# Three waits in front of gathers: tiles 3 to 5 of the feed-forward tail wait for the rows two tiles back

## The reference

```python
x = _layernorm(x + _L0_attn_ref(x, ...))            # causal self-attention, 16 heads of 32
x = _layernorm(x + _L0_xattn_ref(x, ctx_2048, ...)) # 16 heads of 128 on 4 key heads, 361 context rows
x = _layernorm(x + _L0_ffn_ref(x, ...))             # 8 experts, 2 per token

def _L0_ffn_ref(x, router_w, router_b, expert_w, expert_b, proj_w, proj_b, norm_w):
    logits = jnp.einsum('bsd,de->bse', x, router_w) + router_b
    topk_vals, topk_idx = jax.lax.top_k(logits, 2)
    topk_w = jax.nn.softmax(topk_vals, axis=-1)
    full_w = jnp.sum(jax.nn.one_hot(topk_idx, E) * topk_w[..., None], axis=-2)
    h = jnp.einsum('td,edf->etf', xf, expert_w) + expert_b[:, None, :]
    combined = jnp.einsum('etf,te->tf', jax.nn.silu(h), full_w.reshape(-1, E))
    y = x + (combined @ proj_w + proj_b)
    rms = jnp.sqrt(jnp.mean(y * y, axis=-1, keepdims=True) + 1e-6)
    return norm_w * (y / rms)
```

## Time and profile before

| | us |
|---|---|
| median of 3 runs | 1625.73 |
| lowest and highest | 1622.57, 1629.63 |
| the profiled execution | 1628.02 |
| its span, first to last instruction | 1626.2 |
| first gather of the tail to the end of the span | 81.1 |
| GpSimd: gathers of tiles 0 to 6 issued | 1545.1 to 1562.4 |
| GpSimd: `rms(0)` | 1564.4 |

### The profile page before, as it was taken

One profiled execution on the slowest core, in us unless ns is written; L12 is line 12 of the kernel. 1 busy time (PEld: TensorE's weight loads), 2 busy tenths in 40 slices (PEclk: granted clock), 3 DMA queues, 4 the chain that ended last, 5 costly groups with the idle time before them and its releaser, 6 DMA issues. The chain is left out here.

```text
span 1626.2 us, 27742 instructions
## 1 busy us (share of the span) xinstructions
PE 1482.5 (91%) x8494; PEld 1217.7 (75%) x8494; DVE 970.8 (60%) x3587; ACT 655.5 (40%) x1762; POOL 639.2 (39%) x994
## 2 busy tenths in 40 slices
PE   7999999999995689999999999999999998479876
PEld 6778878778764478888888888888888887458754
DVE  3666566666664475556655566555665565744468
ACT  4443343344331254443444444344444444433344
POOL 1334333343342364444443444434344342262173
PEclk8999999999998789999999999999999999579988
DMA  6311212212212441112111111211112110756472
GB/s 204 107 67 62 100 60 78 86 58 81 81 51 86 150 132 42 60 54 64 56 45 59 54 59 39 67 59 54 53 42 68 53 43 21 293 139 167 138 223 81
DMA packets 60957, 139.75 MB, mean 86 GB/s; under 512 B 10182, under 2 KB 21034, under 8 KB 59876
## 3 DMA queue, kind: packets, MB, share of 16 engines
q1 hardware_dynamic: 56296, 123.85, 22.9%
q0 software_dynamic: 4576, 14.95, 3.7%
HBM read 94.31 MB, written 44.46 MB: 85 GB/s over the span
## 5 line engine op out<-in xcount | busy, mean ns | idle before, releaser
L913 ACT ACTIVATE b_probs<-b_probs,b_nmax 100x361 f32<-100x361 f32 x256 | 151.9, 593 | 70.7 <-DVE b_nmax L1011 70.4
L65 PE MATMUL b_bank<-b_kTh,b_q 128*100 128x362 f32 x512 | 174.3, 341 | 3.0 <-DVE b_kTl L993 1.7
L1123 POOL TENSOR_TENSOR b_pcarry<-b_half 128x1 f32<-128x1 f32 x176 | 41.7, 237 | 327.5 <-DVE b_rinv L1017 271.7
L1011 DVE CUSTOM_DVE_ANT_0 b_probs<-b_bank,b_mask 100x361 f32<-100x361 f32 x256 | 135.5, 529 | 56.9 <-issue 46.9
L1148 POOL TENSOR_SCALAR b_probs<-b_probs,b_rinv 100x361 f32<-100x361 f32 x256 | 157.4, 627 | 0.0
L1004 DVE TENSOR_TENSOR b_pTl<-b_bank,b_pTh 121x400 fp32r<-121x400 f32 x192 | 110.0, 573 | 52.6 <-ACT b_pTh L908 51.3
L908 ACT ACTIVATE b_pTh<-b_bank 121x400 fp32r<-121x400 f32 x192 | 96.8, 504 | 102.1 <-PE b_bank L754 99.9
L949 ACT ACTIVATE b_oTh<-b_bank,b_bv 128x400 fp32r<-128x400 f32 x64 | 38.1, 595 | 210.2 <-PE b_bank L65 210.2
L754 PE MATMUL b_bank<-b_ident,b_probs 100*121 100x100 f32 x768 | 110.4, 266 | 5.8 <-POOL b_probs L1148 5.8
L754 PEld LDWEIGHTS b_bank<-b_ident,b_probs 100*121 100x121 f32 x768 | 108.4, 187 | 8.2 <-POOL b_probs L1148 7.3
L65 PE MATMUL b_bank<-b_Woh,b_oTh 128*100 128x512 f32 x256 | 108.0, 422 | 1.4 <-DVE b_oTl L1078 1.4
(11 more groups left out here) (241 smaller groups left out, 3981.1 us busy)
## 6 DMA issues: line engine op xcount, KB each, us to landing
q_d<-a_qo SPq DMA_DIRECT2D x64, 400.0 KB, 2.4
b_q<-q_d SPq DMA_DIRECT2D x64, 400.0 KB, 3.1
b_ctxr<-in_ctxT SPq DMA_DIRECT2D x48, 242.0 KB, 4.0
c_Eraw<-in_expert_w SPq DMA_DIRECT2D x16, 512.0 KB, 11.2
y_d<-c_y SPq DMA_DIRECT2D x32, 256.0 KB, 3.6
a_stage<-in_Wq SPq DMA_DIRECT2D x4, 1024.0 KB, 4.8
stage<-in_Wo SPq DMA_DIRECT2D x8, 512.0 KB, 3.7
a_xTr<-in_xT SPq DMA_DIRECT2D x8, 400.0 KB
```

Source lines behind the costliest of these rows:

```text
L65: mm = eng.matmul(out, lhsT=l(c), rhs=r(c), start=first and k == 0, stop=last and k == n - 1)
L913: act.activation(p, p, ACT.Exp, scale=-1.0, bias=nmax[:, s % 2, h:h + 1], accum_out=psums[:, s % 2, h:h + 1]).then_inc(e_rdy, 1)
L1011: dve.tensor_tensor_reduce(out=probs[:, s % 2, h, 0:SE], in0=s_bank[h % 2][0:S, 0:SE], in1=mask_s[:], scale=-1.0, scalar=BIG, op0=ALU.add, ...
L1123: pool.tensor_tensor(pcarry[:, k:k + 1], half_s[:, 0:1], half_s[:, 0:1], ALU.add)
```

## The change

On GpSimd, in the first of the two loops above, tiles 2, 3 and 4 (the third to fifth) get a wait each ahead of their first gather: for both gathers of tile 0, 1 and 2.

```diff
             for slot in y_out:
                 pool.wait_ge(slot, 16 * NJ // 2)
             for t in range(5):
+                if t >= 2:
+                    pool.wait_ge(r_in[t - 2], 32)
                 gather_results(t)
             for t in range(NT + 2):
                 if t + 5 < NT:
```

## The result

| | us |
|---|---|
| before, median of 20 runs (lowest, highest) | 1629.53 (1622.57, 1633.49) |
| the change, median of 20 runs (lowest, highest) | 1632.41 (1629.16, 1634.87) |
| ratio, 95% interval | 1.0020 (1.0010 to 1.0029) |

The change costs 2.9 us, with an interval from 1.6 to 4.7. That is inside the 0.5% within which I had put it, on the slow side, as forecast; but 1632.41 lies above the upper end of my range, 1631.5. Part of that is the kernel before: over 20 runs its median is 1629.53, where the three runs shown before the prediction gave 1625.73.

The account below looks back on a forecast made before the run. The tail was taken as bound by VectorE's loop over thirteen tiles, started by tile 2's landing. Only tile 4's wait cost anything, 1.6 us, which on the runs' median of 1625.73 gave 1627.3 us, range 1622.5 to 1631.5.

Parts of the forecast that it names:

- Where it happens: GpSimd's three waits: tile 2's and tile 3's cost the end 0, tile 4's delays rms(0) and VectorE's rms_norm(0) by 1.6 us.
- Tile 2 doesn't land sooner: Open term at tile 2's landing: the held-back gathers took no bandwidth from it; gain taken as 0, at most 4.2 us.
- The rival on that landing: Tile 2 lands sooner with fewer gathers under way: half the gain gives 1625.2 us, all of it 1623.1; chance 0.15.
- waits change nothing in sum: Tile 2 usually lands at 1557 or earlier, so GpSimd's idle time swallows tile 4's delay: 1625.7 us; chance 0.12.
- GpSimd blocked by VectorE: One late gather is caught behind a VectorE instruction, +0.5 us: 1627.8 us, or 1628.2 with a dearer wait; chance 0.13.
- Tile 4 too late: Tile 4's gather, issued 3.9 us later behind x2, takes up to 15.4 us: 8.7 us cost, 1634.4 us; chance 0.04.
- the sum: All terms for the tail, 0 + 0 + 1.6 + 0 + 0 = 1.6 us, everything behind rms_norm(0) shifting alike.
- against that I forecast 1627.3: Final step: the 1.6 us laid on the shown runs' median, 1625.73 us, giving 1627.3, range 1622.5 to 1631.5.

Follow-up runs that it names:

- The doses: Two kernels: the change with tile 3 also waiting for tile 2, ratio 1.0035; the kernel before with one wait, between tile 4's two gathers, ratio 1.0003.
- rms_before_gather: The change with all three waits, but from pass 1 on GpSimd does ln and rms before the pass's gather; ratio 0.9997.
- x2_late: The kernel before, without the waits, SyncE issuing the x2 loads only after ScalarE has weighed tile 2, not tile 0; ratio 1.0000.
- again: The change unaltered, timed and profiled a second time against the kernel before; ratio 1.0014 (1.0000 to 1.0028).
- after_fourth: The change unaltered, timed a third time and profiled once more, against the kernel before; ratio 1.0015 (1.0005 to 1.0024).
- late_and_warm: The kernel before, without the waits, with x2 loaded after tile 2 is weighed and 40 unused matmuls before the tail's first transposes; ratio 1.0041.
- warm: The kernel before with 40 matmuls of unused result between the last expert tile and the tail's first transposes; ratio 1.0000.

## Why the prediction was right or wrong

- **Where it happens.** Right. The wait of tile 2 costs 0. That of tile 3 costs 0.39 us on GpSimd (I had 0.21) and nothing behind it. That of tile 4 leaves 3.87 us of idle time and, through six gathers and `rms(0)`, holds VectorE by 1.58 us; I had 1.6. The doses confirm 1.25 us per gather from the sixth on, and rms_before_gather that it is the order on GpSimd that costs. Waking from a wait took 0.24 us (1563.61 to 1563.85), near to the 0.28 of the expert loop.
- **Tile 2 doesn't land sooner.** Right: 13.21 to 14.44 us after the first gather with the change, 13.29 to 14.30 in the kernels without its hold and with x2 loaded early. The Trainium skill ("DMA: Bandwidth & Descriptors", Queues, rings and completion order) says that a DMA engine consumes the descriptors of a ring in order. The landings agree, but they don't prove it: no row shows the rings, and the page says it in its paragraph on the queues of SyncE and ScalarE, which I had carried over to GpSimd's.
- **The rival on that landing was mispriced.** I took every microsecond by which tile 2 lands sooner as a gain for the loop, up to 4.2. x2_late brought 3.8 and the loop gained 0.6, since TensorE's first products come next. So the gains behind the two times of that rival, 1625.2 and 1623.1, were not to be had with the clock as it was, and the lower part of my range leaned on them.
- **The rival "waits change nothing in sum"** is wrong as well: the landing of tile 2 does wander, by over a microsecond, but the hold goes with it, 8.07 or 8.08 in four of five profiles. With x2 loaded early tile 2 never landed sooner than 13.2 us after the first gather, and the rival needed 11.9 (1557).
- **GpSimd blocked by VectorE.** It happens now and then: in again, the gather at 1568.02 came while `combine(3)` was running (from 1567.64, for 0.75 us) and took 1.20 us, and the hold is 8.33, 0.25 more. The Trainium skill ("SBUF — State Buffer", on the shared port pair) says that the one of the two that starts second blocks, and the rows agree; I had priced it at 0.5.

```profile
1567.64 0.75 DVE L1602 SCALAR_TENSOR_TENSOR c_r<-c_r,c_pick 128x512 f32<-128x512 f32 x1 [1.41 <-ACT c_r L1436]
```

```profile
1568.02 1.20 POOL L1690 DMA_INDIRECT c_r<-y_d,c_pick  x1 [0.30 <-issue]
```

- **Tile 4 too late.** Didn't happen: in the profile after, no gather took over 7.5 us (the slowest in the four profiles of the change took 8.2, and it was tile 2's, not tile 4's), and ScalarE never waited for that tile in any profile of the change.
- **What the sum lacked.** I followed the hold to the engines behind VectorE as a plain shift ("All of it shifts by the same 1.6 us, and TensorE and ScalarE with it"). A shift of TensorE is an idle stretch, and in after_fourth its clock fell behind one and 0.7 us more was lost. It also took TensorE as ready whenever tile 2 lands; the profile after has `residual(1)` 0.56 us later than the one before, by TensorE.
- **The step that failed** is the last one, "against that I forecast 1627.3", with its range up to 1631.5. The sum was laid on the median of three runs, 1625.73, and I let a median of a few runs move by some 3 us. Twenty runs put the kernel before at 1629.53, 3.8 us above those three. The profiled execution, 1628.02, had been the better anchor: 1629.6 with the same sum. On 1629.53 the same forecast would have been 1631.1, and 1632.41 is 1.3 above that. So the miss of 5.1 us is 3.8 of baseline and 1.3 of cost, and my allowance of 3 us for the median was smaller than the baseline's part alone. There is chance in it too: in two later sets of twelve runs the change had medians of 1630.25 and 1629.74, inside the range, beside 1627.64 and 1627.72 for the kernel before. The term itself came out as forecast in the trace; by the timed runs the cost is 2.7 to 2.9 us, of which about one is not accounted for by the hold, and is not clear of the scatter; its cause stays open.

## What to carry to other kernels

A wait that is put ahead of a DMA issue holds everything behind it on that engine, also the small operation that another engine needs. What it costs is the delay of that operation, less the time in which it would have lain idle; count the issues between the wait and it, and put the small operation ahead of them where its input is there. When the forecast effect is smaller than the scatter of single runs, lay it on the profiled execution and on the runs together, and give the range the width of the baseline.

## What was not expected of the hardware

- After 1.56 us without work TensorE's granted clock fell from 1.00 to 0.50 for some 3 us in one profile, and stayed at 1.00 in two others after 1.58 and 1.55 us at the same place in the program. After 2.20 us of idle time behind 9 us of gapless matmuls and four transposes (late_and_warm) the products again came one every 0.43 us and not 0.23, and after 1.89 us in `warm` too.
- The part of the program ahead of the tail, the same instructions each time, took from 1541.2 to 1550.8 us over seventeen profiles, while the hold between two instructions of different engines repeats to 0.02 us (6.48 to 6.50 in the seven profiles in which neither the waits nor the late x2 move it).
